# Attention and mixture of experts on one core: the down product one step earlier, and sends that leave out padding

## What is computed

```python
scores = jax.nn.softmax(xt @ Wg.T, axis=-1)            # xt: 2048 x 256, 16 experts
# ... the best 2 of 4 groups of experts, and in them the 4 best experts
combine = jnp.zeros((T, E), xt.dtype).at[jnp.arange(T)[:, None], topi].add(weights)
h = jax.nn.silu(jnp.einsum('td,eid->eti', xt, W1)) * jnp.einsum('td,eid->eti', xt, W3)
expert_out = jnp.einsum('eti,edi->etd', h, W2)         # W1, W3: 176 x 256 for each expert
y = jnp.einsum('etd,te->td', expert_out, combine)
z = jax.nn.silu(xt @ Ws1.T) * (xt @ Ws3.T) @ Ws2.T
```

## Time and profile before

| | us |
|---|---|
| median of 3 runs | 397.82 (397.6 to 398.34) |
| the profiled execution | 396.75 |
| its span, first to last instruction | 395.0 |
| PE busy | 385.2 (98%) |
| DVE busy | 244.3 (62%) |
| POOL busy | 178.6 (45%) |
| ACT busy | 162.8 (41%) |
| bytes moved by DMA | 84.14 MB |

### The profile page before, as it was taken

One profiled execution on the slowest core, in us unless ns is written; L12 is line 12 of the kernel. 1 busy time (PEld: TensorE's weight loads), 2 busy tenths in 40 slices (PEclk: granted clock), 3 DMA queues, 4 the chain that ended last, 5 costly groups with the idle time before them and its releaser, 6 DMA issues.

```text
span 395.0 us, 8998 instructions
## 1 busy us (share of the span) xinstructions
PE 385.2 (98%) x2146; PEld 280.1 (71%) x2147; DVE 244.3 (62%) x676; ACT 162.8 (41%) x494; POOL 178.6 (45%) x225
## 2 busy tenths in 40 slices
PE   7999999999999999999999999999999999999996
PEld 6788888888888646555667675446777777777765
DVE  3577577987988465788735434444445554646465
ACT  5347656564564463101124333333333333334431
POOL 3164323337888574565553333333333333334334
PEclk9999999999999999999999999999999999999999
DMA  7974574358878996256267973334374637363748
GB/s 255 367 245 138 161 280 145 133 201 284 305 255 318 416 420 273 92 208 225 92 197 243 322 238 114 102 116 135 122 250 138 237 116 242 114 231 109 267 112 302
DMA packets 37812, 84.14 MB, mean 213 GB/s; under 512 B 5680, under 2 KB 25616, under 8 KB 35728
## 3 DMA queue, kind: packets, MB, share of 16 engines
q1 hardware_dynamic: 31248, 64.83, 49.3%
q0 software_dynamic: 6528, 18.88, 12.2%
HBM read 60.21 MB, written 23.48 MB: 212 GB/s over the span
## 4 chain that ended last, share of the span: by engine, by line
PE 78%; DVE 11%; DMA 4%; issue 2%; ACT 2%; POOL 0%; DVEq 0%; SPq 0%; POOLq 0%; ACTq 0%
PE heads L1381 18%; PE bank L1455 13%; PE heads L1270 11%; PE heads L1423 7%; PE heads L1272 5%; PE bank L1436 5%; PE bank L1402 4%; PE heads L1391 4%; DVE kv L733 3%; PE bank L1284 3%; PE heads L1373 3%; DMA y_scratch<-toep,dest_i 2%; PE bank L1447 2%; DVE prod L762 2%; DMA xn_tr_all<-y_scratch 2%
## 5 line engine op out<-in xcount | busy, mean ns | idle before, releaser
L716 POOL DMA_INDIRECT y_scratch<-toep,dest_i x72 | 70.2, 975 | 112.9 <-DVE dest_i L1130 95.2
L1381 PE MATMUL heads<-experts,toep 128*128 x256 | 86.5, 461 | 0.6 <-DVE toep L1088 0.5
L1270 PE MATMUL heads<-toep,kv 128*128 128x256 f32 x256 | 77.9, 386 | 1.9 <-DVE kv L733 1.3
L661 POOL DMA_INDIRECT rows_scratch<-rows,slot_i x64 | 63.2, 988 | 35.6 <-issue 19.6
L1455 PE MATMUL bank<-experts,toep 88*128 x256 | 66.1, 381 | 1.2 <-DVE toep L1095 1.2
L553 ACT ACTIVATE toep<-heads 128x176 f32<-128x176 f32 x72 | 22.8, 317 | 77.9 <-PE heads L1381 68.1
L1381 PEld LDWEIGHTS heads<-experts,toep 128*128 128x128 f32 x256 | 43.7, 190 | 14.7 <-issue 1.1
L1272 PEld LDWEIGHTS heads<-toep,kv 128*128 128x128 f32 x256 | 48.7, 190 | 6.5
L762 DVE TENSOR_TENSOR prod<-heads,ctx_rep 128x1024 f32<-128x1024 f32 x32 | 39.1, 1221 | 22.3 <-PE bank L1284 19.9
L1095 DVE COPY toep<-heads 88x256 f32<-88x256 f32 x72 | 30.2, 420 | 31.8 <-PE heads L1391 31.5
L1272 PE MATMUL heads<-toep,kv 128*128 128x128 f32 x256 | 49.2, 274 | 0.0
(11 more groups left out here) (240 smaller groups left out, 500.0 us busy)
## 6 DMA issues: line engine op xcount, KB each, us to landing
ctx_rep<-ctxr_in SPq DMA_DIRECT2D x16, 1024.0 KB, 5.0
experts<-experts_in SPq DMA_DIRECT2D x16, 608.0 KB, 15.4
toep<-rows_scratch SPq DMA_DIRECT2D x56, 144.0 KB
prod<-y_scratch SPq DMA_DIRECT2D x5, 1024.0 KB, 5.6
rows_scratch<-pad_row SPq DMA_DIRECT2D x17, 144.0 KB, 1.8
ctx_tr<-ctxt_in SPq DMA_DIRECT2D x16, 128.0 KB, 5.1
toep<-toep_in SPq DMA_DIRECT2D x4, 512.0 KB, 6.9
ctx_n<-ctx_in SPq DMA_DIRECT2D x16, 128.0 KB, 2.0
```

Source lines behind the costliest of these rows:

```text
L661: pool.indirect_dma_start(rows_d, bass.IndirectOffsetOnAxis(ap=slot_i[:, u, k:k + 1].bitcast(U32), axis=0), rows[:, u, :], None).then_inc( ...
L716: pool.indirect_dma_start(y_d, bass.IndirectOffsetOnAxis(ap=dest_i[b][:, 0:1].bitcast(U32), axis=0), y_sb[b], None).then_inc(y_sent[b], 16)
L1270: nc.tensor.matmul(y_ps[par][:, i, :], kv[:, q, 0, h * P:(h + 1) * P], toep[:, q * HH + h, :], start=True, stop=False)
L1381: last = nc.tensor.matmul(up_ps[p], x_tr[p][:, blk, :], up_w(e, blk), start=blk == 0, stop=blk == LB - 1)
```

## The change

Three things are changed.

1. `down` of a tile is done in the step behind its `up` and no longer two steps behind: step t does `down(t - 1)`. ACT's `store_y` follows it. At the end one `down` is left over where two were.
2. `turn_h(t - 1)` is no longer the last thing of step t: it stands between the two halves of `up(t)`. On DVE `copy_h(t - 1)` now stands ahead of `hidden(t)`.
3. The indirect send gets a bound: destinations behind the last real row are left out, without an error.

```diff
@@ ACT: routed_step
-                if not (isinstance(t, int) and t < 2):
-                    store_y(t - 2, p, (b - 2) % DEPTH, before if b >= 2 else before - 1)
+                if not (isinstance(t, int) and t == 0):
+                    store_y(t - 1, 1 - p, (b - 1) % DEPTH, before if b >= 1 else before - 1)
@@ POOL: send
                     y_d, bass.IndirectOffsetOnAxis(ap=dest_i[b][:, 0:1].bitcast(U32), axis=0),
-                    y_sb[b], None).then_inc(y_sent[b], 16)
+                    y_sb[b], None,
+                    bounds_check=TOPK * TOK - 1, oob_is_err=False).then_inc(y_sent[b], 16)
@@ DVE: routed_step
                 take(t, b, before)
+                if not (isinstance(t, int) and t == 0):
+                    copy_h(t - 1, 1 - b % 2)
                 hidden(t, b % 2, b)
                 if isinstance(t, int) and t < 2:
                     add_z(UNITS - 2 + t)
-                if not (isinstance(t, int) and t == 0):
-                    copy_h(t - 1, 1 - b % 2)
                 place(t, b, before)
@@ PE: up (the mixed form has the same two lines)
                 for blk in range(LB):
+                    if blk == 1 and not (isinstance(t, int) and t == 0):
+                        turn_h(t - 1, 1 - p)
                     last = nc.tensor.matmul(up_ps[p], x_tr[p][:, blk, :],
                                             up_w(e, blk),
@@ PE: routed_step
-                elif not (isinstance(t, int) and t == 1):
-                    if isinstance(t, int) and t < 4:
-                        pe.wait_ge(z_added, UNITS - 3 + t)
-                    down(t - 2, p, (b - 2) % DEPTH)
-                if not (isinstance(t, int) and t == 0):
-                    turn_h(t - 1, 1 - p)
+                else:
+                    if isinstance(t, int) and t < 3:
+                        pe.wait_ge(z_added, UNITS - 2 + t)
+                    down(t - 1, 1 - p, (b - 1) % DEPTH)
             turn_h(LIVE - 1, (LIVE - 1) % 2)
-            for t in range(LIVE - 2, LIVE):
-                down(t, t % 2, t % DEPTH)
+            down(LIVE - 1, (LIVE - 1) % 2, (LIVE - 1) % DEPTH)
```

More of the change, by code:

```diff
@@ L594, in routed_step @@
                     src_tr(t + 1, 1 - p)
-                if not (isinstance(t, int) and t < 2):
-                    store_y(t - 2, p, (b - 2) % DEPTH, before if b >= 2 else before - 1)
+                if not (isinstance(t, int) and t == 0):
+                    store_y(t - 1, 1 - p, (b - 1) % DEPTH, before if b >= 1 else before - 1)
             routed(act, routed_step, 2 * DEPTH)
-            for t in range(LIVE - 2, LIVE):
-                store_y(t, t % 2, t % DEPTH, t // DEPTH)
+            store_y(LIVE - 1, (LIVE - 1) % 2, (LIVE - 1) % DEPTH, (LIVE - 1) // DEPTH)
             for i in range(2):
@@ L1372, in up @@
                     for blk in range(LB):
+                        if blk == 1:
+                            turn_h(t - 1, 1 - p)
                         nc.tensor.matmul(up_ps[p][0:HALF], x_tr[p][:, blk, 0:HALF],
```

## The result

The changed kernel takes 413.51 us (median of 4 runs, 413.12 to 414.0), the kernel before took 397.71 beside it (4 runs, 397.58 to 398.34): a ratio of 1.039, interval 1.037 to 1.041, so 3.9% slower. The forecast was 414.0. The profiled execution took 413.12 for a span of 411.4, 16.4 more than the 395.0 of before; the sum had said 16.3.

A forecast was written before the change was run, and what follows sets the result against it. PE, busy 98% of the span, bounds the kernel. Terms -1.6 + 10.4 + 1.1 + 4.0 + 0.6 + 1.7 + 0.1 = +16.3 us, on the median of 397.82: 414.1, said as 414.0; range 405 to 420.

The forecast's parts named there:

- The copy's wait: Between turn and down: `copy_h` takes 1.20 us against 1.04 of cover, so 61 normal steps wait 0.17 each, +10.4 us.
- The loop, 5.1: Steps 28 to 59: address work behind down's wait adds 1.1 us, the branch in 8 rounds adds 4.0.
- x: Copy of turned x before the next up: 1.16 us against 1.25 of cover, so hidden; at worst 3.7 us, in the range.
- Mixed steps, 0.6: Steps mixing 64 and 128 columns of weights: turning inside up adds four changes at the edges, +0.6 us.
- Lists, 2.1: DVE's two lists behind `place`: the next copy comes late by 1.4 and 0.7 us; net +1.7.
- Waits that go: PE's and DVE's old waits vanish with down one step earlier: -1.6 us, and 0.4 that the lists cost before.
- The end: Around the last up: moved down adds 0.9 ahead; behind it the 1.09 wait for rows read back goes, net -0.8.
- The bound, 0: Indirect sends with a bound: 1 MB of 84 not written, any cost hidden behind POOL's slack, 0 us.
- PE's waits for `copy_h` should be the longest: Sign in the profile after: the longest of PE's waits, 61 times, each some 0.1 to 0.3 us.
- PE's share should fall to about 94%: Sign in the profile after: PE's busy share of the span falls from 98% to about 94%.
- no rival: Alternatives: only the copy's wait paid (0.15), a second operand late (0.14), the wait hidden (0.06), hardly anything (0.02).
- the two large terms: Down's wait for `copy_h` in 61 normal steps, +10.4 us, and the loop's address work and branches, 5.1 us.

The follow-up runs named there:

- the early load: The changed kernel with the number of the expert loaded one tile ahead, before the wait at down: 413.18 us, ratio 1.034.
- the order alone: The kernel before with the turn between the up halves and DVE's order of the change, down still two steps behind: 405.4 us, ratio 1.018.
- the turn first: The changed kernel with the turn at the head of the step, ahead of the first up half, down still one step behind: 434.14 us, ratio 1.089.
- all operands eased: The changed kernel with copies of turned product and x in halves, expert's number loaded one tile ahead, DVE's sums spread: 404.26 us, ratio 1.013.

## Why the prediction was right, point by point

- **The copy's wait, 0.17 x 61.** Right: 0.165 in straight code, with the two links as read from the earlier trace rows (0.26 from copy to load, 0.10 for the load). The Trainium skill, "TensorE: Matmul & The Clock Gate", "Step-by-step: what each phase is for", has weight loads taken ahead of products in flight. By that alone the step would be an estimated 0.10 shorter, 2.56. The trace has 2.655, with down's load 0.25 to 0.28 behind the copy in 58 of 61 steps, so it does not agree where a wait stands ahead of the load.
- **The loop, 5.1.** Right in size, and shown by the early load, which gave back 4.6. By parts it was off: a step with a branch has 0.4 over 2.655, the step behind it 0.1 to 0.3, and the others 0.03 to 0.1, where the forecast had 0.5 for the branch and 0.035 for each step.
- **x, "covered because of the new wait; at worst 0.06 a step".** It was covered, so the sum holds. But the price of it alone was mis-sized: the term is 0.12 a step in straight code, as the order alone showed. The cover was counted right, the way is 1.10 + 0.10 = 1.20 and not 1.16, so it was covered by 0.04 and not by 0.09. I had expected nothing from the order alone, where this term decided in the straight code.
- **Mixed steps, 0.6.** 0.8 for steps 16 to 24. **Lists, 2.1.** 4.15 and 3.11 in the trace of after, 1.49 + 0.45 = 1.94 over 2.66.
- **Waits that go, 1.6 and 0.4 of the lists.** DVE's waits for sends are gone from the list of waits. Steps 4, 10, 14, 35 and 36 of before, 1.6 over their neighbours in all, are in line with theirs now, but for the lists. A little less than 2.0.
- **The end, "+0.9 - 0.8 = +0.1".** Both halves failed and in part cancelled. The down that moved ahead cost 0.1 and not 0.9: in step 1, where it now stands, the kernel before took 2.29 us without any down, since it waited for something else, and the changed one 2.55 with it. Behind the last up 0.3 was won and not 0.8. DVE's last add does end 9.3 behind it instead of 10.3, but the chain through the last turn, copy, down and the sums on PE is later than that, at 408.20, so that the last work of any engine ends 9.64 behind the last up instead of 10.30. And from there the output's transfers and the close take 3.16 us, where before they took 2.77; nothing here shows why.
- **The bound, 0.** Right for the steps, by two runs; the times of these runs are too disturbed to show it.
- **"PE's waits for `copy_h` should be the longest" and "PE's share should fall to about 94%".** Both wrong, though the time was there: 97%, and 3 waits of 2.4 us. Gaps of 0.17 between products disappear in the modelled ends of the products. Step distances and mean durations were the right signs.

So no rival came in. The terms were each within 0.4 us but for the two halves of the end, and those fell in opposite directions. That the two large terms were right is no luck, since the runs that eased them gave most of them back; that the sum met the span to 0.1 us is luck.

## What to carry to other kernels

Where one engine is full, a shorter pipeline has only that engine's few waits to win, and each operand that it makes fresh must be costed as a way, here transposes, copy, 0.26 to the load and 0.10 for the load, against the work that stands between. Ask also what the engine's own instruction stream does behind each wait, since loads of numbers and address work that ran ahead of it for nothing come to stand on the path: 5 us here, and some 30 us with the turn first. Judge a change of a few microseconds by its steps too: four of the runs here missed their expected time while their steps were as expected. And when one late operand is mended, look for the next, which it was hiding.

## What the runs showed of the hardware

- A wait placed ahead of PE's register load can cost far more than the wait: 0.73 us from the turn's weight load to that of up, against 0.18 with the load of the number, its address work and the wait for x moved ahead.
- The way from a semaphore to a weight load was 0.24 to 0.26 us where a copy was late (two engines, four kernels); in the loop of the kernel with the order alone it was 0.13 to 0.14, and there one entry of PE's sequencer stands between the copy's end and the load, where straight code has two.
- PE's idle time of about 3 us was followed by a granted clock of 0.65 to 0.78 in the next stretches of 3 us, in a run where it was 1.00 before; in the runs with all operands eased and without the bound, a stretch stood at 0.50, the lower of its two levels.
- An indirect send of 128 rows took GpSimd 0.98 us with a bound and 0.96 without, and the rows left out are not moved: the queue's bytes fell from 18.88 to 17.84 MB.
